# Layer 3 of a graph network: the gated messages summed in f32 by TensorE, with an f32 copy of the one-hot, in place of a sum of three bf16 parts

## The reference, cut to what matters

```
k = x @ W_key + b_key
q = x @ W_query + b_query
v = x @ W_value + b_value
gate = jax.nn.sigmoid(k[dst] + q[src])
msg = gate * v[src]
agg = jax.ops.segment_sum(msg, dst, num_segments=N_NODES)
return agg + x @ W_skip + b_skip
```

## Time and profile before

| what | us |
|---|---|
| median of 3 runs | 5276.46 (5270.39 to 5276.75) |
| the profiled execution, its own time | 5276.83 |
| its span, first to last instruction | 5274.8 |
| PE busy | 4474.7 (85%) |
| DVE busy | 3575.7 (68%) |
| ACT busy | 2488.1 (47%) |
| POOL busy | 2635.9 (50%) |
| mean granted clock of TensorE | 0.933 |

### The profile page before, as it was taken

How to read it: one execution, slowest core, us unless ns; L and a number is a source line. 1 busy time by engine, 2 the same in 40 slices (tenths; PEclk the granted TensorE clock), 3 DMA queues, 4 the chain that set the end, 5 groups by cost and what they waited for, 6 DMA issues and landing times.

```text
span 5274.8 us, 160095 instructions
## 1 busy us (share of the span) xinstructions
PE 4474.7 (85%) x61948; PEld 4075.5 (77%) x61948; DVE 3575.7 (68%) x5668; ACT 2488.1 (47%) x3821; POOL 2635.9 (50%) x2387
## 2 busy tenths in 40 slices
PE   1777799969999849999999999999758888888587
PEld 1666788869999848888888888888557777777577
DVE  6999888841110247767676767767459999999812
ACT  0333799940000146656565656666235555555400
POOL 0488655556666766666667666661003333333200
PEclk9677899989999979999999999999769999999888
DMA  5996688899999665555555555554045444554396
GB/s 122 222 223 142 219 320 320 321 284 406 377 418 417 256 208 171 163 173 164 172 171 166 171 158 176 169 165 145 26 136 159 154 152 152 152 150 150 106 365 269
DMA packets 802884, 1105.90 MB, mean 210 GB/s; under 512 B 428155, under 2 KB 708081, under 8 KB 794988
## 3 DMA queue, kind: packets, MB, share of 16 engines
q1 hardware_dynamic: 721658, 986.29, 56.9%
q0 software_dynamic: 73696, 111.71, 6.7%
q10 hardware_dynamic: 7056, 0.91, 0.1%
HBM read 788.30 MB, written 314.35 MB: 209 GB/s over the span
## 4 chain that ended last, share of the span: by engine, by line
PE 53%; issue 18%; DVE 11%; DMA 7%; POOL 6%; ACT 4%; SPq 1%; DVEq 0%; POOLq 0%; ACTq 0%
PE PS L1060 10%; PE PS L1169 8%; PE PS L1145 8%; PE PS L1149 8%; PE PS L1156 7%; POOL arena L696 6%; PE PS L1097 3%; PE PS L1128 3%; PE PS L996 2%; DMA arena<-cnt_t 2%; DVE arena L1748 2%; ACT arena L1351 1%; PE PS L835 1%; ACT arena L1355 1%; PE PS L1005 1%
## 5 line engine op out<-in xcount | busy, mean ns | idle before, releaser
L762 POOL DMA_INDIRECT feat_slot<-SK,sidx_p x1764 | 2124.6, 1204 | 1120.0 <-DMA feat_slot<-SK,sidx_p 613.1
L1145 PE MATMUL PS<-arena 128*128 128x128 bf16 x14406 | 1448.3, 221 | 82.7 <-DVE arena L1987 57.5
L1149 PE MATMUL PS<-arena 128*128 (+2 forms) x14406 | 1407.4, 207 | 2.5 <-issue 2.5
L1145 PEld LDWEIGHTS PS<-arena 128*128 128x128 bf16 x14406 | 983.7, 99 | 97.0 <-issue 78.9
L1149 PEld LDWEIGHTS PS<-arena 128*128 128x128 bf16 x14406 | 951.2, 99 | 3.4 <-issue 3.2
L696 POOL TENSOR_TENSOR arena<-arena 128x448 bf16<-128x448 f32 x343 | 359.4, 1048 | 1024.7 <-ACT arena L1463 1024.7
L2007 DVE TENSOR_TENSOR arena<-arena 128x896 f32<-128x896 f32 (+1 forms) x686 | 586.2, 855 | 390.8 <-ACT arena L1454 385.2
L1169 PE MATMUL PS<-arena 128*128 128x384 bf16 (+1 forms) x4802 | 708.0, 288 | 146.8 <-POOL arena L696 143.6
L1463 ACT ACTIVATE arena<-arena 128x896 bf16<-128x896 f32 (+1 forms) x686 | 523.7, 763 | 561.5 <-DVE arena L2007 559.2
L1060 PE MATMUL PS<-arena 128*128 128x192 bf16 (+1 forms) x7203 | 613.9, 248 | 106.7 <-DVE arena L1845 62.3
L1060 PEld LDWEIGHTS PS<-arena 128*128 128x128 bf16 x7203 | 605.8, 98 | 113.5 <-DVE arena L1845 62.7
(11 more groups left out here) (238 smaller groups left out, 5778.8 us busy)
## 6 DMA issues: line engine op xcount, KB each, us to landing
arena<-slot_rows SPq DMA_DIRECT2D x1372, 224.0 KB
arena<-cnt_t SPq DMA_DIRECT2D x147, 896.0 KB
arena<-cnt_t SPq DMA_DIRECT2D x147, 672.0 KB
feat_slot<-zero SPq DMA_DIRECT2D x7, 10976.0 KB, 115.8
cnt_t<-arena SPq DMA_DIRECT2D x49, 1568.0 KB
cnt_s<-arena SPq DMA_DIRECT2D x49, 1568.0 KB
arena<-feat_slot SPq DMA_DIRECT2D x343, 224.0 KB
SK<-in_edge_attr_dram POOLq DMA_DIRECT2D x196, 288.0 KB
```

The lines of the kernel that those rows point to most:

```text
L762: pool.indirect_dma_start(feat_slot, bass.IndirectOffsetOnAxis(ap=sidx_p[odd][:, n:n + 1].bitcast(u32), axis=0), fwin[h][:, t * D:(t + 1) ...
L1145: last = nc.tensor.matmul(PS[:, to:to + P], selS[c][:, cut], qsplit[:, (b * 3 + s) * H:(b * 3 + s + 1) * H], start=s == 0 and (k != 4 or j ...
L1149: last = nc.tensor.matmul(PS[:, to:to + w_], selT[c][:, cut], dsplit[:, bass.ds(w * (3 * w_) + s * w_, w_)], start=False, stop=k != 4 and ...
```

## The change

In layer 3 the message stays f32. `add_messages` on PE multiplies an f32 one-hot, `sumF[i]`, with `hid[i]`: 7 matmuls, 64 f32 columns each, where `add_up` had 7 with 192 bf16 columns. ACT makes `sumF[i]` from `sumT[c]` (896 elements, bf16 to f32); it has two buffers in room that only layer 2 uses. The bf16 copies on ACT, the residual on DVE and POOL's part of the layer are gone. The sigmoid of a chunk now waits until the sums of the chunk two before are made. `first_part` and `second_part` move 64 columns in place of 192, with one addition in place of three. Layer 2 keeps its code.

```diff
+        sumF = [carve(110.25 + 3.5 * i, CH * P) for i in range(2)]
...
-            def last_parts():
-
-                n = CH * W_TAB[5]
-
-                def body(w, odd, first=False):
-                    for c in range(NC):
-                        i = (c + odd) % 2
-                        pool.wait_ge(msg_mid, w * NC + (GB + c + 1))
-                        pool.tensor_tensor(parts3[i][:, 2 * n:3 * n], hid[i][:, 0:n], parts3[i][:, n:2 * n], ALU.subtract)\
-                            .then_inc(msg_lo, 1)
-                blocks(pool, body)
...
+                def add_messages(w, c, odd):
+
+                    half, i = int(c >= 4), (c + odd) % 2
+                    if c in (0, 4):
+                        pe.wait_ge(zb_kept if half else za_kept, w + NB)
+                    pe.wait_ge(pre_free, w * NC + (GB + c + 1))
+                    pe.wait_ge(msg_hi, w * NC + (c + 1))
+                    o = PS[:, 3072 + half * 512:3072 + half * 512 + D]
+                    for j in range(CH):
+                        last = nc.tensor.matmul(o, sumF[i][:, j * P:(j + 1) * P], hid[i][:, j * D:(j + 1) * D],
+                                                start=c in (0, 4) and j == 0, stop=c in (3, 6) and j == CH - 1)
+                    last.then_inc(agg_made, 1)
...
-                        act.wait_ge(msg_lo, n + (GB - 1))
+                        act.wait_ge(agg_made, n + (GB - 1))
...
-                        act.wait_ge(pre_free, w * NC + (GB + c + 1))
-                        if later(w, c, 2):
-                            act.wait_ge(agg_made, w * NC + (GB + c - 1))
-                        nc.scalar.activation(parts3[i][:, 0:n], hid[i][:, 0:n], ACT.Copy).then_inc(msg_hi, 1)
-                        if more:
-                            gates_of(w * NC + (c + 1), 1 - i)
...
+                    if k == 5:
+                        gates_of(w * NC + c, i)
+                        act.wait_ge(sel_made, w * NC + (GB + c + 1))
+                        nc.scalar.activation(sumF[i], sumT[c], ACT.Copy).then_inc(msg_hi, 1)
+                        return
...
                 def residual(w, c, odd):
 
                     i = (c + odd) % 2
-                    dve.wait_ge(*((pre_free, w * NC + (c + 1)) if k == 4 else (msg_hi, w * NC + (c + 1))))
+                    if k == 5:
+                        return
+                    dve.wait_ge(pre_free, w * NC + (c + 1))
...
+                    if k == 5:
+                        V.tensor_tensor(ystage[:, 0:w_], y0[:, 0:w_], PS[:, 3584:3584 + w_], ALU.add).then_inc(zb_kept, 1)
+                        return
```

More of the change, by code:

```diff
@@ L791, in _ @@
             for k in range(7):
-                if k == 5:
-                    with pool.If(fast):
-                        last_parts()
                 with pool.If(1 - fast):
@@ L1440, in gates_of, with messages @@
                         .then_inc(gate_made, 1)
-                def messages(w, c, odd, more=True):
+                def messages(w, c, odd):
                     i = (c + odd) % 2
@@ L1446, in messages @@
                     n = CH * w_
-                    if k == 4:
-                        act.wait_ge(pre_made, w * NC + (c + 1))
-                        if later(w, c, 2):
[L1450 to L1455, removed]
-                        act.wait_ge(pre_free, w * NC + (GB + c + 1))
-                        if later(w, c, 2):
-                            act.wait_ge(agg_made, w * NC + (GB + c - 1))
-                        nc.scalar.activation(parts3[i][:, 0:n], hid[i][:, 0:n], ACT.Copy).then_inc(msg_hi, 1)
-                        if more:
-                            gates_of(w * NC + (c + 1), 1 - i)
-                    act.wait_ge(msg_res, w * NC + (m * GB + c + 1))
+                    if k == 5:
[3 more added lines that the diff above has]
+                        return
+                    act.wait_ge(pre_made, w * NC + (c + 1))
+                    if later(w, c, 2):
+                        act.wait_ge(msg_lo, w * NC + (c - 1))
+                    nc.scalar.activation(hid[i], PS[:, at:at + CH * P], ACT.Relu)
+                    if later(w, c, 2):
+                        act.wait_ge(agg_made, w * NC + (c - 1))
+                    nc.scalar.activation(parts3[i][:, 0:n], PS[:, at:at + CH * P], ACT.Relu).then_inc(pre_free, 1)
+                    act.wait_ge(msg_res, w * NC + (c + 1))
                     nc.scalar.activation(parts3[i][:, n:2 * n], hid[i][:, 0:n], ACT.Copy).then_inc(msg_mid, 1)
@@ L1468, in first_part @@
                     act.wait_ge(agg_made, w * NC + (m * GB + 4))
-                    nc.scalar.activation(y0[:, 0:3 * w_], PS[:, 3072:3072 + 3 * w_], ACT.Copy).then_inc(za_kept, 1)
+                    n = 3 * w_ if k == 4 else w_
+                    nc.scalar.activation(y0[:, 0:n], PS[:, 3072:3072 + n], ACT.Copy).then_inc(za_kept, 1)
                 def body(w, odd, first=False):
@@ L1478, in body @@
                     first_part(w)
-                if k == 5:
-                    gates_of(0, 0)
                 blocks(act, body)
                 messages(NB - 1, NC - 2, 0)
-                messages(NB - 1, NC - 1, 0, False)
+                messages(NB - 1, NC - 1, 0)
             def fast_or_general(k):
@@ L2024, in second_part @@
                     dve.wait_ge(za_kept, w + (m * NB + 1))
-                    n = w * 2 + (m * 2 * NB)
+                    n = w * 2
+                    if k == 5:
+                        V.tensor_tensor(ystage[:, 0:w_], y0[:, 0:w_], PS[:, 3584:3584 + w_], ALU.add).then_inc(zb_kept, 1)
+                        return
                     V.tensor_tensor(y0[:, 0:3 * w_], y0[:, 0:3 * w_], PS[:, 3584:3584 + 3 * w_], ALU.add).then_inc(y_step, 1)
```

1 line of the change is left out of this document (added).

## The result

The change is slower: 5429.93 us median of 4 runs (5411.05 to 5441.31) against 5276.37, a ratio of 1.0287 with a 95% interval of 1.0265 to 1.0308. That is 154 us more, where 163 were forecast.

The account below looks back on a forecast made before the run. DVE, delayed by POOL, bounds layer 3's slot pass before; PE's f32 sums after. Stage 343 x 3.45 = 1183 + 35 + 3 = 1221 us against 1058.0, so 5276 + 163 = 5439 us, range 5375 to 5495.

Parts of the forecast that it names:

- The bound and its change: Layer 3's slot pass: DVE bounds at 2.87 us a chunk before; PE bounds after, at 3.45, without gaps.
- The f32 sums, 14 x 0.112 = 1.57 us: PE, layer 3: seven f32 sums a chunk are 14 records of 0.112 us, priced by L874, replacing 0.58 us.
- The gap of 0.04 us before the sums: PE, between meet and sums: 0.04 us a chunk for the longer f32 weight load, added to 1.84.
- the two meets before the first sums: PE, after each loop stop: two meets of 1.79 us each at the lower clock, 3 us no longer covered.
- The stops, five of 7 us: Ends of PE's eight-block loop in layer 3: five stops of some 7 us, idle time and lower clock, 35 us.
- The sum: Layer 3's stage: 343 x 3.45 = 1183 + 35 + 3 = 1221 us against 1058.0, 163 us slower.
- The chain over ACT and DVE, with 2 us to spare: Sums, ACT's sigmoid, DVE's product, then meet: about 1.15 us plus hand-overs, hidden behind PE's 3.45 us.
- DVE at 2.1 us a chunk, ACT at 1.49: Layer 3: DVE falls from 2.87 to about 2.1 us; ACT's widening copy and sigmoid take 1.49, hidden.
- two of the signs: Signs expected in the after profile: DVE near 65% busy in the stage, and a block at 24.2 us.
- The rival by columns: Columns set PE's f32 price: sums 0.80 us, stage 944, kernel 5162 us; chance 0.05, 0.01 more within 0.2%.
- The clock that stays down: Rival: PE stays at half clock after stops, some 3.2 us more a chunk, 5600 to 6350 us; chance 0.07 over 5495.

Follow-up runs that it names:

- both longer runs: Two of the four runs of the change itself, nothing altered, near 5441 us; the other two were near 5415.
- the run with the long loop: The change with PE's loop of layer 3 24 blocks long in place of 8: 5387.23 us median, the stage 1168.2 us.

## Why the prediction was right

*The bound and its change:* right. DVE was it before, held up by POOL; PE is it after, without a gap.

*The f32 sums, 14 x 0.112 = 1.57 us:* measured 1.59. This term carried the forecast. It came from the one line in the trace with the same shape in both operands: L1156, at 0.083 with more columns, would have misled by 0.4 us a chunk. The experiments show that the weight columns had to be the same, and that the moving columns need not have been. Why L1156, on 64 partitions, costs less, no run here shows.

*The gap of 0.04 us before the sums:* mis-sized. From meet to sums it is 1.78 us, not 1.84 + 0.04. The 1.84 of before held about 0.05 us of gap that I took for a need of PE's: without POOL's part the kernel before has 1.785 in most chunks too, and the forecast itself took 1.79 for the two meets before the first sums. The chunk is 3.375 us, not 3.45: 26 us less over 343 chunks.

*The stops, five of 7 us:* 9.1 each (9.3 by the chunks around them), 11 us more. The price came from layer 2. After a stop in layer 3 the meet begins at a granted clock of 0.50, after four of the five the next sums begin at it as well (0.50 from 4344, 4544, 4744 and 4942 us, 1.00 from 4148 after the first), and PE has nothing in hand to make up for it.

*The sum:* 148.6 us for the stage where 163 stood. The median's 154 has a few more, which fits the clock of layer 2's projections if both longer runs had it. That the profiled execution hit 5441 against 5439 is part luck: two errors of the sum, -26 and +11, and 16 us from another stage.

*The chain over ACT and DVE, with 2 us to spare:* right. In the chunk shown above, the product that follows the sums ended at 4522.90 is over at 4524.30, and the meet that needs it begins at 4526.27, 1.97 us later. With bf16 sums most chunks took 1.98 us, so it did not bind there either.

*DVE at 2.1 us a chunk, ACT at 1.49:* DVE's 57.70 us in 100 are 1.95 us a chunk, and 942 + 543 ns for ACT. So two of the signs came out lower than written: DVE was busy for 55% of the stage (667.8 of 1206.6 us) and not near 65, and a block takes 7 x 3.375 = 23.6 us and not 24.2.

*The rival by columns:* refuted in the sizes 32, 64 and 128, at 0.112, 0.114 and 0.117 us a record. Whether the columns set the price beyond 128, no run here shows. *The clock that stays down:* it did not come; with f32 sums in nearly half of each chunk the clock stood at 1.00 between stops (4200 to 4300 us, above) and at 0.98 over the stage. Where it did stay down was in f32 projections: in layer 3's, at 0.50 from 3830 to 3870 us as in the kernel before, and in this execution in layer 2's too.

## What to carry to other kernels

Price a matmul by a line of the trace that has the same type, the same partitions, weight columns and moving columns. In f32 a matmul here was two records with a weight load each, 0.11 us apart for 128 weight columns, so few moving columns make it dear: 64 f32 columns cost 0.23 us a matmul, 192 bf16 columns 0.08. Splitting into bf16 parts on other engines looks roundabout, and here it is cheaper for PE. Where a change moves the bound from one engine to another, apply it to a fraction of the work, so that both come out even: two chunks of seven gained 80 us, where all seven lost 154.

## What the runs showed that I had not expected

- A bf16 matmul of 64 columns with a new 128x128 weight load costs 0.20 / 7 = 0.029 us, a quarter of one f32 record of the same shape. I had expected twice as much.
- Each jump back of PE's loop cost 9.6 us by the run with the long loop and 9.1 in the profile of the change, of which 4.2 to 5.6 us are idle and the rest is the lower clock after it (0.50 from 4340 to 4348 us after the second).
- In layer 2's projections, f32 on 65 partitions, PE is busy without a gap and yet the granted clock is at 0.50 for 50 us in two of twelve profiles and at 1.00 in the others, worth 20 us on that line. Layer 3's projections, the same shapes, ran at the low clock in all twelve (43.0 or 43.1 us). What decides it no run here shows.
- POOL's subtraction slowed DVE in a second place, the once-a-block addition of two SBUF operands: 968 ns with it, 224 without.
